# Making a unit's second diagonals on ScalarE instead of GpSimd, from unit 8 on

## The chip, the cores and the metric

The kernel runs on one core of one Trainium2 chip. Its time is the device time of one execution in microseconds (us), given as the median of three runs. A core has five engines that run their own instruction streams and meet only at semaphores: TensorE (PE in the profile, with its weight loads as PEld), VectorE (DVE), ScalarE (ACT), GpSimd (POOL) and SyncE (SP), which here only issues DMAs.

## The reference, cut to what matters

Four blocks are added one after the other to `x` (4 batches, 256 rows, 256 columns): a recurrence, a quantised feed-forward layer, a grouped attention over two sets of keys, and a routed linear attention. The change lies in the third block, whose core is:

```python
def _gqa(q, k, v):
    scale = 1.0 / np.sqrt(q.shape[-1])
    scores = jnp.einsum('bsghd,btgd->bghst', q, k) * scale
    p = jax.nn.softmax(scores, axis=-1)
    return jnp.einsum('bghst,btgd->bsghd', p, v)

q = _ln(_fp8_linear_pertensor(ln_out, wq, ...)); k = _ln(...); v = ...
core = _gqa(q, k, v)            # x = 0 in the kernel
qx = _ln(...); kx = _ln(...); vx = ...
xout = _gqa(qx, kx, vx)         # x = 1 in the kernel
```

There are 4 batches with 8 groups of 2 heads each, and each group has both attentions.

## The kernel before, in words

A **unit** is one group of one batch; there are 32, numbered 0 to 31, and unit u = 8 b + g. Within a unit `x` is 0 for the first attention and 1 for the second, and `t` is one of two tiles of 128 rows. The order of the work is written out by hand, one list for each engine; nothing is reordered. An engine that waits holds up everything behind it in its own list.

What a unit's second half of the pipeline does:

- `guard(u, x)` on TensorE (L700) makes scores in bfloat16, only to find the largest score of each row; `maxima(u, x, t)` on VectorE (L1852) takes the negated maximum into `nm`.
- `diagonals(u, x)` (L1426) turns `nm` into four 128x128 diagonal matrices in `diag`, by multiplying an identity matrix `identb` with the maximum of each row. In the kernel before, GpSimd makes all of them: one operation of 128x512 for x = 0 and one for x = 1.
- `scores(u, x, t)` on TensorE makes the real scores transposed (L714) and adds the diagonals through a matmul with ones (L715), which subtracts the row's maximum in every column. It waits for `diag_ready`.
- `exps(u, x, t)` on ScalarE (L1109) takes the exponentials, `weigh(u, x, t)` on TensorE (L734) multiplies with the values, and `outputs(u, x, t)` on VectorE (L1865, L1867) divides by the sums into `Cb`.
- `quantise(u - 1)` on VectorE (L1879 to L1883) rounds the unit before to 8 bits in five operations over 128x1024 elements.

Beside this runs the start of the next unit: `project(u + 1, t)` on TensorE (L590 and L597), `squares` and `values` on ScalarE (L1126, L1116), `powers` on GpSimd (L1409, L1411), `normalise` on VectorE (L1840, L1844), `turn` on TensorE (L673) and `evacuate` on ScalarE (L1150). Spread over the eight units of a batch lies the work of the first two blocks of the next batch, and from unit 25 on some preparation of the fourth block.

TensorE's list for a plain unit is scores(u, 0, 0), scores(u, 0, 1), project(u + 1, 1), scores(u, 1, 0), weigh(u, 0, 0), turn_outputs(u - 1), scores(u, 1, 1), weigh(u, 0, 1), turn(u + 1), weigh(u, 1, 0), project_values(u + 2), guard(u + 1, 0), weigh(u, 1, 1), project(u + 2, 0), guard(u + 1, 1). The last unit, 31, has no next one: its four scores stand directly behind each other.

Of the kernel before, what the change touches and what calls it, by code (L numbers as in the profile page):

```python
# [7 lines left out]
ALU = mybir.AluOpType  # L8
ACT = mybir.ActivationFunctionType
# [34 lines left out]
def build_program(nc, a, out):  # L44
# [15 lines left out]
    NT, KT = S // P, D // P  # L60
    HEADS = a["L1_xattn_wq"].shape[0] // P
    G = a["L1_xattn_wk"].shape[0] // P
    HPG = HEADS // G
# [10 lines left out]
    with main:  # L74
# [3 lines left out]
        def sb(name, shape, dt=F32, stack=main):  # L78
            return stack.enter_context(nc.sbuf_tensor(name, shape, dt))
# [7 lines left out]
        identb = sb("identb", [P, P], BF16)  # L87
# [69 lines left out]
        nm = [eb(f"nm{i}", [P, 2, HPG, NT]) for i in range(2)]  # L157
        diag = [eb(f"diag{i}", [P, 2, HPG * NT, P], BF16) for i in range(2)]
# [126 lines left out]
        def heads(buffer, l):  # L285
# [19 lines left out]
            "xq_ready xqT_done xqT_evac ffn_done ffn_read zT_done lnT_evac y4_ready xq4_ready "  # L305

            "qkv_done q1_done v_ready ss_ready root_ready rs_ready norm_done tr_done qt_evac smax_done "
            "max_ready diag_ready st_done exp_done pv_done o_evac cq_ready cT2_done catT_evac proj_done x3_ready "

            "ve3_ready pw3_ready h3_ready h3T_done h3T_evac conv_ready silu_ready proj3_done gate3_done qkv3_evac g3_evac rotated "  # L310
            "th_done sq_ready vs_ready sd_ready sd_done wv3_ready wk3_ready head_rstd_ready og_ready o_ready last_o_ready oT_done oT_evac out_done "
# [3 lines left out]
        s = {n: sem(n) for n in names.split()}  # L315
# [154 lines left out]
        def _(pe):  # L470
# [233 lines left out]
            def scores(u, x, t):  # L704

                n = 4 * u + 2 * x + t
                o = SB[n % 2]
                free(o)
                if n >= 2:
                    pe.wait_ge(s["exp_done"], n - 1)  # L710
                if t == 0:
                    pe.wait_ge(s["qt_evac"], 4 * (u + 1))
                    pe.wait_ge(s["diag_ready"], 2 * u + x + 1)
                nc.tensor.matmul(o[:], KTt[u % 2][:, x, t * P:(t + 1) * P], QT[u % 2][:, x, :], start=True, stop=False)  # L714
                nc.tensor.matmul(o[:], onesb[:], diag[u % 2][:, x].rearrange("p a b -> p (a b)"), start=False, stop=True  # L715
                                 ).then_inc(s["st_done"], 1)
# [260 lines left out]
            u = UNITS - 1  # L977
# [43 lines left out]
        def _(act):  # L1021
            A = nc.scalar.activation
# [80 lines left out]
            def exps(u, x, t):  # L1103

                n = 4 * u + 2 * x + t
                act.wait_ge(s["st_done"], n + 1)
                if u:
                    act.wait_ge(s["pv_done"], 4 * (u - 1) + 2 * x + 2)
                A(Pt[:, x, t], SB[n % 2][:], ACT.Exp, scale=SCALE).then_inc(s["exp_done"], 1)  # L1109

            def values(u, t):

                act.wait_ge(s["qkv_done"], 4 * u + 2 * t + 2)
                if u >= 2 and t == 0:
                    act.wait_ge(s["pv_done"], 4 * (u - 1))
                A(V[u % 2][:, :, t, 0:P], QB[2 * t + 1][:].rearrange("p (x j c) -> p x j c", x=2, j=2)[:, :, 1, :], ACT.Copy  # L1116
                  ).then_inc(s["v_ready"], 1)
# [125 lines left out]
            for u in range(UNITS - 1):  # L1243
                nb, steps = ahead(u)
                exps(u, 0, 0)
                if u == 0:
                    turned_h(1)
                if u >= SCORES_FIRST:
                    exps(u, 0, 1)
                if 7 in steps and u < G:  # L1250
                    over_scales(nb, (0, 1))
                if u + 1 == G:
                    squares(u + 1, 0)
                    values(u + 1, 0)
                    for r in round_of(u, 0):
                        weights(*r)
                squares(u + 1, 1)
                values(u + 1, 1)
                if 7 in steps and u >= G:
                    over_scales(nb, (0, 1))  # L1260
                if 1 in steps:
                    turned_context(nb)
                if 5 in steps:
                    turned_xq(nb)
                if u < SCORES_FIRST:
                    exps(u, 0, 1)
                exps(u, 1, 0)
                if u >= 1 and not (u % G == 1 and u > G) and 4 not in steps:
                    outputs(u - 1)
                exps(u, 1, 1)  # L1270
                if 4 in steps:
                    outputs(u - 1)
                for r in round_of(u, 1 if u + 1 == G else 0):
                    weights(*r)
                if 1 in steps:
                    differences(nb, 0, 1)
                evacuate(u + 1, range(3))
                if u % G == 1 and u > G:
                    outputs(u - 1)
                evacuate(u + 1, (3,))  # L1280
                if 7 in steps and u >= G:
                    over_scales(nb, (2, 3))
                for r in round_of(u, 2 if u + 1 == G else 1):
                    weights(*r)
                if 7 in steps and u < G:
                    over_scales(nb, (2, 3))
                if 1 in steps:
                    differences(nb, 2, 3)
                if 6 in steps and u < G:
                    turned_z(nb)  # L1290
                if u + 2 != G and u + 2 < UNITS:
                    squares(u + 2, 0)
                    values(u + 2, 0)
                if 0 in steps:
                    turned_h(nb)
                if 6 in steps and u >= G:
                    turned_z(nb)
                if u + 1 != G:
                    for r in round_of(u, 2):
                        weights(*r)  # L1300

            u = UNITS - 1
            exps(u, 0, 0)
            exps(u, 0, 1)
            exps(u, 1, 0)
            exps(u, 1, 1)
            outputs(u - 1)
# [36 lines left out]
        def _(pool):  # L1344
# [76 lines left out]
            def diagonals(u, x):  # L1421

                pool.wait_ge(s["max_ready"], 4 * u + 2 * x + 2)
                if u >= 2 and x == 0:
                    pool.wait_ge(s["st_done"], 4 * (u - 1))
                gp.tensor_tensor(diag[u % 2][:, x], identb[:].unsqueeze(1).to_broadcast([P, HPG * NT, P]),  # L1426
                                 nm[u % 2][:, x].rearrange("p h t -> p (h t)").unsqueeze(2).to_broadcast([P, HPG * NT, P]),
                                 ALU.mult).then_inc(s["diag_ready"], 1)

            inv_freq = (1.0 / np.float32(10000.0) ** (np.arange(0, DK3, 2, dtype=np.float32) / np.float32(DK3))).astype(np.float32)  # L1430
            for l in range(B):
# [54 lines left out]
            for u in range(UNITS):  # L1486
                nb, steps = ahead(u)
                diagonals(u, 0)
                if u + 1 != G and u + 1 < UNITS:
                    powers(u + 1, 0)  # L1490
                diagonals(u, 1)
                if 2 in steps:
                    weighted_values(nb)
                if u + 1 == G:
# [61 lines left out]
        def _(dve):  # L1556
# [290 lines left out]
            def maxima(u, x, t):  # L1847

                dve.wait_ge(s["smax_done"], 4 * u + 2 * x + t + 1)
                if u >= 2 and x == 0 and t == 0:  # L1850
                    dve.wait_ge(s["diag_ready"], 2 * (u - 1))
                v.tensor_reduce(nm[u % 2][:, x, :, t], GUARD_BANK[t][:].rearrange("p (h t) -> p h t", h=HPG), AX_X, ALU.max,  # L1852
                                negate=True).then_inc(s["max_ready"], 1)

# [295 lines left out]
            u = UNITS - 1  # L2150
# [75 lines left out]
```

## Time and profile before

| | us |
|---|---|
| median of 3 runs (range) | 662.53 (662.47 to 662.95) |
| the profiled execution's own time | 662.35 |
| its span, first to last instruction | 660.4 |
| TensorE busy | 610.7 |
| VectorE busy | 542.9 |
| ScalarE busy | 402.8 |
| GpSimd busy | 255.9 |

The span lies 1.95 us under the execution's own time, and that is 0.18 us under the median. Busy times of the engines overlap. A matmul's end is modelled by the profile, so two matmuls of one list can seem to overlap; distances between starts are the safer reading.

### The profile page before, as it was taken

To read this page: it belongs to the slowest core of one execution; us is meant where nothing else is said; L and a number is where in the kernel's file an instruction comes from. 1 tells how busy PE (TensorE), PEld (TensorE's weight loads), DVE (VectorE), ACT (ScalarE), POOL (GpSimd) and SP (SyncE) were. 2 spreads that over 40 slices of the span, in tenths; PEclk is the share of its full clock that TensorE was granted. 3 is DMA by queue.
4 is the path that set the end of the run, shared out by engine and by line. 5 is a ranking of instruction groups with operands and counts; after the bars stand their busy time and mean duration, and the time that the engine had idled before them with its cause. 6 is when DMAs were issued, how large, how long until landed. Compare 5 with 4: busy or idle time off the path is not lost.

```text
span 660.4 us, 13262 instructions
## 1 busy us (share of the span) xinstructions
PE 610.7 (92%) x4526; PEld 490.9 (74%) x4567; DVE 542.9 (82%) x1284; ACT 402.8 (61%) x1355; POOL 255.9 (39%) x344
## 2 busy tenths in 40 slices
PE   3567999999899999999999999999999999999957
PEld 2456787777678887787788877887887888887735
DVE  6999788989797879898878798889775777868697
ACT  4468866766676645667567466576553656665632
POOL 2213664343433543343345533333332444431281
PEclk9558999999999999999999999999999999999977
DMA  8486752330653203333343232333342233010001
GB/s 273 141 290 196 244 172 81 100 100 6 222 190 100 106 14 105 103 105 108 103 122 105 94 105 105 104 105 105 106 167 105 105 105 104 17 34 1 1 0 64
DMA packets 36972, 72.86 MB, mean 110 GB/s; under 512 B 3342, under 2 KB 28586, under 8 KB 32810
## 3 DMA queue, kind: packets, MB, share of 16 engines
q1 hardware_dynamic: 36720, 72.00, 33.5%
q8 instruction: 37, 0.61, 0.4%
q14 instruction: 29, 0.24, 0.1%
q10 hardware_dynamic: 186, 0.02, 0.0%
HBM read 59.41 MB, written 12.60 MB: 109 GB/s over the span
## 4 chain that ended last, share of the span: by engine, by line
PE 67%; DVE 25%; issue 4%; ACT 3%; POOL 1%; DMA 0%; POOLq 0%; DVEq 0%
PE bank L734 14%; PE bank L714 13%; PE bank L590 12%; PE bank L597 7%; PE bank L673 4%; PE bank L700 3%; DVE nm L1852 3%; PE bank L758 3%; PE bank L715 2%; DVE Cb L1867 2%; PE bank L748 2%; PE bank L480 1%; PE bank L771 1%; DVE Ce L1880 1%; DVE big L2016 1%
## 5 line engine op out<-in xcount | busy, mean ns | idle before, releaser
L1126 ACT ACTIVATE square<-bank 128x128 bf16<-128x128 f32 x372 | 97.7, 280 | 87.3 <-PE bank L590 72.8
L734 PEld LDWEIGHTS bank<-V,Pt 128*128 128x128 f32 x1024 | 128.2, 191 | 27.0 <-DVE Cb L1867 13.6
L734 PE MATMUL bank<-V,Pt 128*128 128x129 f32 x1024 | 136.3, 276 | 3.7 <-DVE Cb L1867 3.1
L714 PE MATMUL bank<-QT,KTt 128*128 128x512 f32 x256 | 132.5, 599 | 2.0 <-POOL diag L1426 0.3
L1426 POOL TENSOR_TENSOR diag<-identb,nm 128x512 bf16<-128x512 bf16 x64 | 67.7, 1058 | 168.3 <-DVE nm L1852 168.1
L1109 ACT ACTIVATE Pt<-bank 128x512 f32<-128x512 f32 x128 | 76.7, 599 | 67.0 <-remote 37.7
L1852 DVE TENSOR_REDUCE nm<-bank 128x2 f32<-128x512 f32 x128 | 82.3, 684 | 19.6 <-PE bank L700 19.3
L1411 POOL TENSOR_TENSOR rs<-ve,mhalf 128x6 f32<-128x6 f32 x62 | 87.9, 1417 | 5.2
L1867 DVE SCALAR_TENSOR_TENSOR Cb<-bank,ro,ism 128x128 bf16<-128x128 f32 x256 | 78.0, 346 | 4.5
L590 PE MATMUL bank<-WQ,xq 128*128 128x256 f32 x512 | 79.2, 297 | 1.4 <-DVE xq L1761 0.8
L1126 ACT ACTIVATION_READ_ACCUMULATOR square<-bank 128x1 f32 x372 | 78.1, 210 | 0.0
L590 PEld LDWEIGHTS bank<-WQ,xq 128*128 128x128 f32 x512 | 66.8, 189 | 14.6 <-DVE nm L1852 7.0
L597 PE MATMUL bank<-WC,vT 128*128 128x256 f32 x256 | 69.5, 396 | 0.7 <-ACT WC L1096 0.7
L1865 DVE RECIPROCAL ro<-bank 128x2 f32<-128x2 f32 x128 | 21.1, 165 | 56.8 <-PE bank L734 56.6
L1150 ACT ACTIVATE QT<-bank,vec 128x512 f32<-128x512 f32 x64 | 50.1, 783 | 19.8 <-PE bank L673 19.8
L1409 POOL TENSOR_SCALAR ve<-ss 128x6 f32<-128x6 f32 x62 | 17.9, 288 | 112.6 <-ACT square L1126 112.6
L590 PE MATMUL bank<-WH,xh 128*128 128x128 bf16 x768 | 54.1, 220 | 1.5 <-DVE xh L1761 1.5
L714 PEld LDWEIGHTS bank<-QT,KTt 128*128 128x128 f32 x256 | 43.0, 190 | 14.7 <-issue 11.4
L597 PEld LDWEIGHTS bank<-WC,vT 128*128 128x128 f32 x256 | 44.9, 195 | 4.6 <-ACT WC L1096 0.9
L590 PEld LDWEIGHTS bank<-WH,xh 128*128 128x128 bf16 x768 | 43.1, 98 | 4.7 <-DVE xh L1761 1.9
L673 PE MATMUL bank<-ident,Qn 128*128 128x128 f32 x372 | 45.7, 273 | 0.0
L1158 ACT ACTIVATE catT<-bank 128x1024 bf16<-128x1024 bf16 x32 | 32.8, 1024 | 18.7 <-PE bank L748 18.7
(241 smaller groups left out, 1052.0 us busy)
## 6 DMA issues: line engine op xcount, KB each, us to landing
WQ<-wq_split SPq DMA_DIRECT2D x24, 1024.0 KB, 7.7
WH<-wh_split SPq DMA_DIRECT2D x24, 384.0 KB, 8.9
wq_split<-WQ SPq DMA_DIRECT2D x8, 1024.0 KB, 5.2
ism<-smooth_inverse SPq DMA_DIRECT2D x32, 256.0 KB, 6.4
wpst<-in_L_xattn_wproj SPq DMA_DIRECT2D x16, 256.0 KB, 4.6
wh_split<-WH SPq DMA_DIRECT2D x8, 384.0 KB, 5.1
wst<-in_L_xattn_wq SPq DMA_DIRECT2D x8, 256.0 KB, 4.8
wst<-in_L_xattn_wqx SPq DMA_DIRECT2D x8, 256.0 KB, 5.0
```

Of the source, the lines that this page charges most:

```text
L590: last = nc.tensor.matmul(o[:, o0:o0 + n], x, w, start=m == 0, stop=m == parts * KT - 1)
L597: last = nc.tensor.matmul(QB[2 * t + 1][:, 2 * P:4 * P], vT[b % 2][:, k, t * P:(t + 1) * P], WC[:, k, g, :], start=k == 0, stop=k == KT - 1)
L673: last = nc.tensor.transpose(o[:, (j * NT + t) * P:(j * NT + t + 1) * P], Qn[:, t, h, :], ident[:])
L714: nc.tensor.matmul(o[:], KTt[u % 2][:, x, t * P:(t + 1) * P], QT[u % 2][:, x, :], start=True, stop=False)
L734: last = nc.tensor.matmul(o[:, h * (P + 2):h * (P + 2) + P + 1], Pt[:, x, k, h * S + t * P:h * S + (t + 1) * P], V[u % 2][:, x, k, 0:P + 1 ...
L1109: A(Pt[:, x, t], SB[n % 2][:], ACT.Exp, scale=SCALE).then_inc(s["exp_done"], 1)
L1126: last = A(square[:, t, h], head(t, h), ACT.Square, accum_out=ss[:, t, h:h + 1])
L1150: A(o, i, ACT.Identity, scale=vc(f"L1_xattn_{name}ln_w"), bias=vc(f"L1_xattn_{name}ln_b")).then_inc(s["qt_evac"], 1)
L1411: gp.tensor_tensor(rs[:, t, :], ve[:, t, :], mhalf[:, 0:6], ALU.pow).then_inc(s["rs_ready"], 1)
L1426: gp.tensor_tensor(diag[u % 2][:, x], identb[:].unsqueeze(1).to_broadcast([P, HPG * NT, P]), nm[u % 2][:, x].rearrange("p h t -> p (h t)") ...
L1852: v.tensor_reduce(nm[u % 2][:, x, :, t], GUARD_BANK[t][:].rearrange("p (h t) -> p h t", h=HPG), AX_X, ALU.max, negate=True).then_inc(s["ma ...
L1867: last = v.scalar_tensor_tensor(out=c4[:, t, x, h, :], in0=o[:, h * (P + 2):h * (P + 2) + P], scalar=ro[:, x, t, h:h + 1], in1=ism[:, u % ...
```

## The change

For units 8 to 31 the diagonals of x = 1 are made by ScalarE in four operations of 128x128, each a copy of the identity matrix with the column of negated maxima as its scale. They stand in ScalarE's list behind exps(u, 0, 1) and ahead of squares(u + 1, 1); in unit 31 they stand between exps(31, 0, 1) and exps(31, 1, 0). GpSimd keeps the diagonals of x = 0 for all units and those of x = 1 for units 0 to 7. The one semaphore `diag_ready` becomes two, `diag0_ready` and `diag1_ready`.

```diff
@@ TensorE, scores
-                    pe.wait_ge(s["diag_ready"], 2 * u + x + 1)
+                    pe.wait_ge(s[f"diag{x}_ready"], u + 1)
@@ ScalarE
+            def diagonals(u):
+
+                act.wait_ge(s["max_ready"], 4 * u + 4)
+                act.wait_ge(s["st_done"], 4 * (u - 1))
+                for h in range(HPG):
+                    for t in range(NT):
+                        last = A(diag[u % 2][:, 1, h * NT + t, :], identb[:], ACT.Copy, scale=nm[u % 2][:, 1, h, t:t + 1])
+                last.then_inc(s["diag1_ready"], 1)
...
                 if u >= SCORES_FIRST:
                     exps(u, 0, 1)
+                if u >= G:
+                    diagonals(u)
...
             u = UNITS - 1
             exps(u, 0, 0)
             exps(u, 0, 1)
+            diagonals(u)
             exps(u, 1, 0)
             exps(u, 1, 1)
@@ GpSimd
-                                 ALU.mult).then_inc(s["diag_ready"], 1)
+                                 ALU.mult).then_inc(s[f"diag{x}_ready"], 1)
...
-                diagonals(u, 1)
+                if u < G:
+                    diagonals(u, 1)
@@ VectorE, maxima
-                if u >= 2 and x == 0 and t == 0:
-                    dve.wait_ge(s["diag_ready"], 2 * (u - 1))
+                if u >= 2 and t == 0:
+                    dve.wait_ge(s[f"diag{x}_ready"], u - 1)
```

ScalarE's list in unit 22, before. `Pt` is what exps writes, `square` what squares writes, `V1` what values writes:

```order
L1109 ACTIVATE Pt<-bank4 128x512 [waits pv_done,st_done]
L1109 ACTIVATE Pt<-bank5 128x512 [waits pv_done,st_done]
L1126 ACTIVATE square,ss<-bank2 128x128 [waits rs_ready,qkv_done]
L1126 ACTIVATE square,ss<-bank2 128x128 x3
L1126 ACTIVATE square,ss<-bank3 128x128 [waits qkv_done]
L1126 ACTIVATE square,ss<-bank3 128x128
```

The same place after the change; line numbers behind L1110 have moved by 9:

```order
L1109 ACTIVATE Pt<-bank4 128x512 [waits pv_done,st_done]
L1109 ACTIVATE Pt<-bank5 128x512 [waits pv_done,st_done]
L1117 ACTIVATE diag0<-identb,nm0 128x128 [waits st_done,max_ready]
L1117 ACTIVATE diag0<-identb,nm0 128x128 x3
L1135 ACTIVATE square,ss<-bank2 128x128 [waits rs_ready,qkv_done]
L1135 ACTIVATE square,ss<-bank2 128x128 x3
L1135 ACTIVATE square,ss<-bank3 128x128 [waits qkv_done]
L1135 ACTIVATE square,ss<-bank3 128x128
```

Four operations have come between the second exponential and the first squares, and with them a wait for all four maxima of the unit.

ScalarE's list in unit 31, before:

```order
L1109 ACTIVATE Pt<-bank4 128x512 [waits pv_done,st_done]
L1109 ACTIVATE Pt<-bank5 128x512 [waits pv_done,st_done]
L1109 ACTIVATE Pt<-bank4 128x512 [waits pv_done,st_done]
L1109 ACTIVATE Pt<-bank5 128x512 [waits pv_done,st_done]
L1158 ACTIVATE catT<-bank7 128x2x512 [waits cT2_done]
```

and after:

```order
L1109 ACTIVATE Pt<-bank4 128x512 [waits pv_done,st_done]
L1109 ACTIVATE Pt<-bank5 128x512 [waits pv_done,st_done]
L1117 ACTIVATE diag1<-identb,nm1 128x128 [waits st_done,max_ready]
L1117 ACTIVATE diag1<-identb,nm1 128x128 x3
L1109 ACTIVATE Pt<-bank4 128x512 [waits pv_done,st_done]
L1109 ACTIVATE Pt<-bank5 128x512 [waits pv_done,st_done]
L1167 ACTIVATE catT<-bank7 128x2x512 [waits cT2_done]
```

Here the diagonals of x = 1 stand behind the exponentials of x = 0, where GpSimd made them beside these.

GpSimd's list over units 30 and 31, before (`rs` is what powers makes):

```order
L1426 TENSOR_TENSOR diag0<-identb,nm0 128x512 [waits st_done,max_ready]
L1409 TENSOR_SCALAR ve<-ss 128x6 [waits norm_done,ss_ready]
L1411 TENSOR_TENSOR rs<-ve,mhalf 128x6 [waits pool_chain]
L1426 TENSOR_TENSOR diag0<-identb,nm0 128x512 [waits max_ready]
L1409 TENSOR_SCALAR ve<-ss 128x6 [waits norm_done,ss_ready]
L1411 TENSOR_TENSOR rs<-ve,mhalf 128x6 [waits pool_chain]
L1426 TENSOR_TENSOR diag1<-identb,nm1 128x512 [waits st_done,max_ready]
L1426 TENSOR_TENSOR diag1<-identb,nm1 128x512 [waits max_ready]
```

and after:

```order
L1438 TENSOR_TENSOR diag0<-identb,nm0 128x512 [waits st_done,max_ready]
L1421 TENSOR_SCALAR ve<-ss 128x6 [waits norm_done,ss_ready]
L1423 TENSOR_TENSOR rs<-ve,mhalf 128x6 [waits pool_chain]
L1421 TENSOR_SCALAR ve<-ss 128x6 [waits norm_done,ss_ready]
L1423 TENSOR_TENSOR rs<-ve,mhalf 128x6 [waits pool_chain]
L1438 TENSOR_TENSOR diag1<-identb,nm1 128x512 [waits st_done,max_ready]
```

One operation of 128x512 in each unit is gone from the list, 24 in all; the rest has kept its order.

## Rows read from the trace of the kernel before

**Rows 1.** The page, part 1: busy us, share of the span, instructions.
```profile
PE 610.7 (92%) x4526; PEld 490.9 (74%) x4567; DVE 542.9 (82%) x1284; ACT 402.8 (61%) x1355; POOL 255.9 (39%) x344
```

**Rows 2.** Timeline of TensorE: start, us, line, operands, count, [idle before].
```profile
385.25 1.22 PE L590 MATMUL bank<-WQ,xq 128*128 128x256 f32 x8
397.50 1.19 PE L590 MATMUL bank<-WQ,xq 128*128 128x256 f32 x8
...
434.45 1.30 PE L590 MATMUL bank<-WQ,xq 128*128 128x256 f32 x8
...
445.96 1.20 PE L590 MATMUL bank<-WQ,xq 128*128 128x256 f32 x8
450.38 1.21 PE L590 MATMUL bank<-WQ,xq 128*128 128x256 f32 x8
...
457.85 1.16 PE L734 MATMUL bank<-V,Pt 128*128 128x129 f32 x8 [1.10 <-DVE Cb L1867]
...
463.17 1.19 PE L590 MATMUL bank<-WQ,xq 128*128 128x256 f32 x8
```

**Rows 3.** The chain that ended last, in unit 16: start, us, what.
```profile
343.76 0.44 PE bank L480 x4
```

**Rows 4.** Timeline of VectorE, units 18 and 22.
```profile
386.16 1.20 DVE L1880 TENSOR_SCALAR Ce<-Cb 128x1024 uint16<-128x1024 uint16 x1
...
450.84 0.42 DVE L1879 TENSOR_SCALAR Cb<-Cb 128x1024 bf16<-128x1024 bf16 x1
451.30 1.15 DVE L1880 TENSOR_SCALAR Ce<-Cb 128x1024 uint16<-128x1024 uint16 x1
```

**Rows 5.** Line 1880 alone: duration in ns, min/median/max, first and last start.
```profile
L1880 DVE TENSOR_SCALAR Ce<-Cb x32: 426/429/1202, 84.8 to 607.9; 128x1024 uint16<-128x1024 uint16 x32
```

**Rows 6.** Timeline of GpSimd, unit 22.
```profile
451.00 1.15 POOL L1426 TENSOR_TENSOR diag<-identb,nm 128x512 bf16<-128x512 bf16 x1
```

**Rows 7.** Timeline of ScalarE, unit 21.
```profile
434.84 0.60 ACT L1109 ACTIVATE Pt<-bank 128x512 f32<-128x512 f32 x1 [0.48 <-PE bank L715]
435.79 0.28 ACT L1126 ACTIVATE square<-bank 128x128 bf16<-128x128 f32 x1 [0.35 <-PE bank L590]
...
437.40 0.28 ACT L1126 ACTIVATE square<-bank 128x128 bf16<-128x128 f32 x1 [0.47 <-PE bank L597]
...
438.17 1.71 ACT L1050 ACTIVATE tmp<-tmp,vec 128x256 bf16<-128x256 f32 x4
439.77 0.60 ACT L1109 ACTIVATE Pt<-bank 128x512 f32<-128x512 f32 x1
```

**Rows 8.** Timeline of TensorE's weight loads, unit 21.
```profile
436.98 0.41 PEld L714 LDWEIGHTS bank<-QT,KTt 128*128 128x128 f32 x2
```

**Rows 9.** Timeline of ScalarE, in the first batch.
```profile
130.03 1.14 ACT L1092 ACTIVATE WH<-bank,vec 128x128 bf16<-128x128 f32 x4
```

**Rows 10.** Groups by line and form: count, busy us, mean ns, idle before.
```profile
L1109 ACT ACTIVATE Pt<-bank 128x512 f32<-128x512 f32 x128 | 76.7, 599 | 67.0 <-remote 37.7 <-PE bank L715 26.4
...
L1116 ACT ACTIVATE V<-bank 128x256 f32<-128x256 f32 x64 | 25.5, 398 | 0.0
```

**Rows 11.** Timeline of ScalarE, unit 31.
```profile
599.38 0.60 ACT L1109 ACTIVATE Pt<-bank 128x512 f32<-128x512 f32 x1 [0.48 <-PE bank L715]
```

**Rows 12.** The chain that ended last, from unit 31 on.
```profile
598.10 1.02 PE bank L714 x2
599.12 0.22 PE bank L715
599.34 0.86 PE bank L714 x2
600.20 0.21 PE bank L715
...
617.45 0.93 PE bank L864 x4
```

**Rows 13.** Busy time in stretches: PE, PEld, DVE, ACT, POOL, granted clock, DMA.
```profile
594.00:600.00 6.00, 5.86 (x32) 3.51 (x33) 5.86 (x13) 1.47 (x3) 2.19 (x2) 1.00 0.00 0
...
636.00:642.00 6.00, 0.00 (x0) 0.00 (x0) 5.74 (x11) 1.76 (x3) 5.37 (x9) 0.57 0.00 0
642.00:648.00 6.00, 4.97 (x15) 3.77 (x16) 5.83 (x9) 1.29 (x3) 3.70 (x4) 0.50 0.00 1
```

More of the change, by code:

```diff
@@ L307, in build_program @@
             "qkv_done q1_done v_ready ss_ready root_ready rs_ready norm_done tr_done qt_evac smax_done "
-            "max_ready diag_ready st_done exp_done pv_done o_evac cq_ready cT2_done catT_evac proj_done x3_ready "
+            "max_ready diag0_ready diag1_ready st_done exp_done pv_done o_evac cq_ready cT2_done catT_evac proj_done x3_ready "
             "ve3_ready pw3_ready h3_ready h3T_done h3T_evac conv_ready silu_ready proj3_done gate3_done qkv3_evac g3_evac rotated "
```

## The prediction

> **What bounds the kernel now.** I read the busy shares first. TensorE is busy for 92% of the span [rows 1], so time can be saved only where it stands still, and it is lost wherever TensorE is made to stand still. Then I looked for such places in units 8 to 31, by the distance between the starts of equal matmuls in TensorE's timeline. From the second project of a unit to the first project of the next-but-one there are 11.51 us in a plain unit: 434.45 to 445.96 in unit 21 [rows 2]. In unit 22 the same list takes 12.79 us, 450.38 to 463.17, though no matmul is added; 1.28 us are lost. The row at 457.85 shows where: weigh(22, 0, 1) waits for VectorE's output. In unit 18 it is 12.25 us, 385.25 to 397.50 [rows 2]; four transposes belong to that unit alone, at 0.44 us [rows 3], so 12.25 - 11.51 - 0.44 = 0.30 us are lost. Units 14 and 10 repeat 22 and 18 one batch earlier, with the same distances. Elsewhere in units 8 to 31 I find next to nothing lost behind the second diagonals.
>
> Then VectorE in those units. It works without a pause in unit 22, and one operation of quantise sticks out: L1880 took 1.15 us at 451.30, in unit 18 it took 1.20 us at 386.16 [rows 4], while its median over the kernel is 0.43 [rows 5]. GpSimd was making the second diagonals meanwhile, from 451.00 to 452.15 [rows 6], and L1880 ends 0.30 us behind that. L1879, just ahead, took 0.42 us beside a ScalarE exponential. So a fast operation of VectorE stands still while GpSimd's operation runs, and not while ScalarE's does.
>
> The Trainium skill has a rule for this: "GPSIMD Engine Reference", section on specifications, says that GpSimd's interfaces to SBUF are shared with VectorE, with contention against instructions in a two-port mode or with two SBUF inputs. The trace agrees for L1880, by the 1.15 us above against 0.43.
>
> **What the change removes.** 24 GpSimd operations of some 1.04 to 1.15 us. GpSimd is busy for 39% [rows 1] and nobody waits there, so this by itself is worth 0; what stood behind it in GpSimd's list, powers(u + 1, 1) and in units 9 and 17 a product for the next batch, may start 1 us earlier, where TensorE loses nothing. With each goes a stall of VectorE of about 0.72 us (1.15 - 0.43), some 17 us of VectorE's time. TensorE collects it only where it waits behind that stall:
> - units 14 and 22: the stall of 0.72 is smaller than the 1.28 us lost, so all of it counts: 2 x 0.72 = 1.44 us;
> - units 10 and 18: 0.77 (1.20 - 0.43) is more than the 0.30 lost, so TensorE becomes the limit and only 0.30 counts: 2 x 0.30 = 0.60 us;
> - the 20 other units: TensorE does not wait behind this stall, 0.
>
> Saved: 2.04 us. The bound below is 0 (another wait takes the place at once), the bound above is all that is lost in the four, 2 x 1.28 + 2 x 0.30 = 3.2 us.
>
> **What the change adds: the length of the four copies.** The trace has no operation of just this form. The nearest is L1050, a copy from SBUF to SBUF in bfloat16 with a scale from a column, but of 256 columns: four took 1.71 us [rows 7]. The exponentials of 512 columns take 599 ns and the values' copies of 256 take 398 [rows 10], so 128 columns are worth about 0.10 us, and four shorter copies take 1.71 - 4 x 0.10 = 1.31 us. L1092 has 128 columns and a scale column but reads PSUM; four took 1.14 us [rows 9]. I take 1.31, since its source lies in SBUF as here. Bounds: 1.14 below and 1.71 above. On ScalarE the next operation starts about 0.11 us before the last has ended (438.17 + 1.71 against 439.77 [rows 7]).
>
> **In units 8 to 30** the copies fall into a pause. In unit 21 the second exponential starts at 434.84 and takes 0.60; the squares start at 435.79, and the fifth square at 437.40 after another pause of 0.47 us, each time on TensorE's project [rows 7]. With the copies: they run from 435.33 to 436.64, the squares start at 436.53 instead of 435.79, four squares take about 1.0 us (436.53 to 437.53), and the fifth starts some 0.1 us late instead of waiting 0.47. Two who might wait: scores(u, 1, 0) needs the diagonals, and its weights are loaded at 436.98 [rows 8], 0.34 us behind their end; and GpSimd's powers, VectorE's normalise and TensorE's turn hang on the squares, late by 0.1 us, where VectorE had other work to do first. The maxima that the copies wait for are made about when the second exponential is done. Cost 0 each; with copies of 1.71 us in all they would end at 437.04, still about when the weights are loaded, so 0 to 0.1 each.
>
> The new wait of maxima(u, 1, 0) on VectorE, ahead of all its later work, is for diagonals of two units ago, some 30 us old: 0.
>
> **In unit 31** there is no project between the scores, and this cover is gone. Before, GpSimd made the diagonals beside the exponentials. Now exps(31, 0, 1) runs at 599.38 for 0.60 us [rows 11], the copies from 599.87 to 601.18, and about 0.06 us later TensorE may start scores(31, 1, 0), at 601.24. Its two matmuls then take 1.02 us as they do behind a wait (598.10 [rows 12]) and end at 602.26, where they ended at 599.34 + 0.86 = 600.20 before. Everything behind is late by 2.06 us, and nothing absorbs it: the chain of waits is TensorE without a gap from 599.34 to the row at 617.45 [rows 12], and goes on from its result. Bounds: 1.14 makes it 1.89, 1.71 makes it 2.46.
>
> **The sum.** -2.04 + 0 + 2.06 = +0.02 us. The profiled execution has 662.35 us, so 662.37; the median of the runs stood 0.18 above it, so I forecast 662.5 us. The case's own range, from the bounds that go together, is 661.2 (3.2 saved, 1.89 lost) to 663.6 (1.44 saved, 2.46 lost).
>
> **Rivals.**
> - *Another wait takes the place, and the last unit pays alone.* VectorE's stall goes in unit 22, but TensorE then waits there as long for the exponentials or for the squares that ScalarE now makes later. Against it: ScalarE had pauses of 0.48, 0.35 and 0.47 us in such a unit [rows 7]. Time: 662.53 + 2.06 = 664.6. This is slower. Chance 0.10.
> - *The copies outlast the window in every unit.* From the second exponential's start to the weights of scores(u, 1, 0) there are 436.98 - 434.84 = 2.14 us [rows 7, 8]; 0.49 go to the exponential, so the copies may take 1.65 us, 0.41 each. Beyond that TensorE waits in each of the units 8 to 30, 23 at most. At 1.85 us: 23 x 0.2 = 4.6, and 2.6 in unit 31, less 2.04: 667.7. Four operations of 128 columns in 1.14 us, 0.29 each, speak against it [rows 9]. Chance 0.04.
> - *The clock falls in unit 31.* The granted clock is 1.00 from 594 to 600, and fell to 0.57 and 0.50 of full speed (the lower level, 1.2 GHz, is 0.50) in the stretches from 636 and from 642, after TensorE had done nothing for 6 us [rows 13]. The new pause in unit 31 is near 2 us, longer than the 1.10 us at 457.85 and shorter than that one. If the clock fell for 6 us, TensorE would do half the work in them, about 3 us more: 665.5. Chance 0.04.
> - *The tail takes it in.* The last unit's wait is hidden, since VectorE and ScalarE behind it have pauses, and the savings stand alone: 662.53 - 2.04 = 660.5. The gapless chain [rows 12] speaks against it. Together with savings at their upper bound that I have not found the places for, chance 0.12.
> - *The change does nothing*, if VectorE's stall is not GpSimd's doing and the last unit's copies are hidden by something: 662.5, the same number; it lies within the chance of the first case.
>
> The rule that speaks loudest against this change is that of the clock: the Trainium skill, "TensorE: Matmul & The Clock Gate", part 1, says that a monitor halts every second pulse when TensorE has not been busy lately. The trace agrees by the 0.57 behind the idle stretch from 636; by the rule the third rival's time would be right only if the new pause counts as idle, and no run here shows one of 2 us.
>
> **How the numbers follow.** What a measurement of this kernel can tell from no change is 0.2%, 1.3 us, so faster means under 661.2 and slower over 663.9. The forecast has 0.70, and nearly all of it lies within. The faster rival gives 0.12. The slower ones give 0.10 + 0.04 + 0.04 = 0.18. The range takes in the first rival's 664.6 above and, below, a little more than the case's own bound of 661.2: 661.0 to 664.6, with under 0.2 left outside.
>
> **What would show it.** The second operation of quantise on VectorE, L1880 before, at 0.43 us in nearly every unit from 8 on. The project distance of units 14 and 22 near 12.07 instead of 12.79, of units 10 and 18 near 11.95. ScalarE's four copies at about 1.3 us in the pause behind the second exponential, with the fifth square starting at most 0.1 us behind TensorE. TensorE idle for 1.9 to 2.5 us ahead of the third scores of unit 31, released by ScalarE, and the clock at 1.00 there. I am wrong if TensorE waits for ScalarE's diagonals in other units, if unit 22 stays at 12.79, or if the last unit shows no new pause.

## The result, and the profile after

Over 20 runs of each kernel the changed one takes 664.75 us (663.18 to 666.68) and the one before 662.54 us (662.44 to 664.40). The ratio is 1.0035 with a 95% interval of 1.0024 to 1.0046: slower by 2.2 us, where I had forecast 662.5 and at most 664.6. The 20 runs stand in three levels, which the explanation needs: five lie at 663.18 to 663.30, seven at 664.67 to 664.81, eight at 666.22 to 666.68. The profiled execution took 664.69 us.

Part 1 of its page, against [rows 1]:

```profile
PE 610.6 (92%) x4526; PEld 489.9 (74%) x4567; DVE 525.3 (79%) x1284; ACT 426.2 (64%) x1451; POOL 230.1 (35%) x320
```

VectorE lost 542.9 - 525.3 = 17.6 us of busy time with the same 1284 instructions, GpSimd 25.8 us with 24 fewer. The stalls went as forecast. Line numbers of VectorE stand 13 further on in this kernel (they move by 9 only in ScalarE's part): L1893 is L1880 of before, and L1880 is the old L1867. The same places as [rows 4], VectorE's timeline in units 18 and 22 (start, us, line, operands):

```profile
385.46 0.43 DVE L1893 TENSOR_SCALAR Ce<-Cb 128x1024 uint16<-128x1024 uint16 x1
...
450.48 0.43 DVE L1893 TENSOR_SCALAR Ce<-Cb 128x1024 uint16<-128x1024 uint16 x1
```

The second operation of quantise, L1893 now, takes 0.43 where it took 1.20 and 1.15. In the kernel before, each of the units 8 to 31 had exactly one lengthened operation of quantise beside the second product of GpSimd, but not always this one: it was L1880 in 11 units, L1881 in 3 and L1882 in 10. So the sign that I had named, L1880 at 0.43, held in 13 of the 24 units already before; the sum of 17.6 us is the better sign. In unit 21 of the kernel before the lengthened one was L1882, whose median is 0.69:

```profile
434.38 1.41 DVE L1882 TENSOR_TENSOR Cb<-Cb,Ce 128x1024 bf16<-128x1024 bf16 x1
```

TensorE's timeline in the changed kernel, beside [rows 2]:

```profile
384.55 1.22 PE L590 MATMUL bank<-WQ,xq 128*128 128x256 f32 x8
396.69 0.48 PE L590 MATMUL bank<-WQ,xq 128*128 128x256 f32 x2
...
449.57 1.21 PE L590 MATMUL bank<-WQ,xq 128*128 128x256 f32 x8
...
456.31 1.16 PE L734 MATMUL bank<-V,Pt 128*128 128x129 f32 x8 [0.38 <-DVE Cb L1880]
461.64 1.19 PE L590 MATMUL bank<-WQ,xq 128*128 128x256 f32 x8
```

Unit 22 takes 12.07 us (12.79 before) and the wait for VectorE is 0.38 (1.10 before): 0.72 us won, as forecast; unit 14 won 0.71. Unit 18 takes 12.14 us (12.25 before): 0.11 won, where I had 0.30; unit 10 won 0.10. Together these are 1.64 us.

ScalarE in unit 21, the place of [rows 7]:

```profile
434.03 0.60 ACT L1109 ACTIVATE Pt<-bank 128x512 f32<-128x512 f32 x1 [0.48 <-PE bank L715]
434.52 1.26 ACT L1117 ACTIVATE diag<-identb,nm 128x128 bf16<-128x128 bf16 x4
435.69 0.26 ACT L1135 ACTIVATE square<-bank 128x128 bf16<-128x128 f32 x1
...
436.69 0.29 ACT L1135 ACTIVATE square<-bank 128x128 bf16<-128x128 f32 x1
```

The four copies take 1.26 us (forecast 1.31) and lie in ScalarE's pause. The fifth square, at 436.69, starts 2.66 us behind the second exponential where it was 2.56 [rows 7]: 0.10 late, as forecast. The view of line 1117 alone (duration in ns min/median/max, first and last start; then who waited for it, us and times) says that TensorE waited for it once in 24 units:

```profile
L1117 ACT ACTIVATE diag<-identb,nm x96: 386/390/403, 210.5 to 599.2; 128x128 bf16<-128x128 bf16 x96
...
  PE bank L714: 1.9, 1
```

That once is unit 31. ScalarE's and then TensorE's timeline there:

```profile
597.86 0.60 ACT L1109 ACTIVATE Pt<-bank 128x512 f32<-128x512 f32 x1 [0.47 <-PE bank L715]
598.36 1.26 ACT L1117 ACTIVATE diag<-identb,nm 128x128 bf16<-128x128 bf16 x4
```

```profile
599.76 1.44 PE L714 MATMUL bank<-QT,KTt 128*128 128x512 f32 x2 [1.94 <-ACT diag L1117]
600.99 0.63 PE L715 MATMUL bank<-diag,onesb 128*128 128x512 bf16 x1
601.42 1.91 PE L714 MATMUL bank<-QT,KTt 128*128 128x512 f32 x2
603.13 0.63 PE L715 MATMUL bank<-diag,onesb 128*128 128x512 bf16 x1
603.55 1.18 PE L734 MATMUL bank<-V,Pt 128*128 128x129 f32 x8
604.57 0.61 PE L748 MATMUL bank<-identb,Cb 128*128 128x128 bf16 x8
```

The pause of 1.94 us is the one that I worked out. What follows it is not: the two pairs of L714 behind the wait take 1.44 and 1.91 us, where the same pairs behind the same wait take 1.10 and 1.02 at full clock (experiment 9), and L715 takes 0.63 instead of 0.38. The stretches of this time (PE, PEld, DVE, ACT, POOL busy, then the granted clock) say why:

```profile
600.00:602.00 2.00, 2.00 (x4) 0.80 (x4) 0.00 (x0) 0.33 (x1) 0.00 (x0) 0.60 0.00 0
602.00:604.00 2.00, 2.00 (x6) 0.93 (x5) 0.00 (x0) 0.46 (x2) 0.00 (x0) 0.55 0.00 0
604.00:606.00 2.00, 2.00 (x24) 1.99 (x23) 1.09 (x5) 1.18 (x2) 0.00 (x0) 1.00 0.00 0
```

Finer stretches of the same trace have 0.50 (the lower level, 1.2 GHz) or 1.00 (2.4 GHz), and a value between them where the clock changes within the stretch. At 0.60 and 0.55 the clock was at the lower level for (0.40 + 0.45) x 2.00 / 0.50 = 3.4 us. The finer ones put this at 600.4 to 603.8: the first matmuls behind the pause, from 599.76, still ran at full clock. From the chain that ended last (start, us, what), against the 617.45 of [rows 12]:

```profile
598.36 1.27 ACT diag L1117 x4
...
599.76 1.44 PE bank L714 x2
...
619.80 0.93 PE bank L864 x4
```

The end of unit 31's work is late by 619.80 - 617.45 = 2.35 us, which is the whole difference of the two profiled executions (664.69 - 662.35 = 2.34). At unit 30's start the changed kernel was 1.52 us ahead (584.10 before, 582.58 after: 1.64 saved less 0.12 by which the first units of the two executions differ), so unit 31 cost 2.35 + 1.52 = 3.87 us. The pause's part is read from an execution with full clock (the faster one of experiment 9): there weigh(31, 0, 0) starts 6.55 us behind the unit's first scores, before it was 4.37, so the pause and its restart cost 2.18 us. The other 1.7 us are the clock's.

### The profile page after: what moved, and what is told of

It is laid out like the page before. It is cut to its first block, busy times and chain, and to the rows that moved or that the text cites. A ratio compares the mean times of both kernels' runs of the same rounds, so it can differ in the third digit from the quotient of the medians.

```text
span 662.7 us, 13383 instructions
## 1 busy us (share of the span) xinstructions
PE 610.6 (92%) x4526; PEld 489.9 (74%) x4567; DVE 525.3 (79%) x1284; ACT 426.2 (64%) x1451; POOL 230.1 (35%) x320
## 4 chain that ended last, share of the span: by engine, by line
PE 70%; DVE 21%; issue 4%; ACT 3%; POOL 1%; DMA 0%; DVEq 0%; POOLq 0%; ACTq 0%
PE bank L734 15%; PE bank L714 14%; PE bank L590 13%; PE bank L597 7%; PE bank L673 5%; PE bank L700 3%; PE bank L758 3%; DVE nm L1865 2%; PE bank L715 2%; PE bank L748 2%; DVE Cb L1880 1%; PE bank L480 1%; PE bank L771 1%; DVE big L2029 1%; DVE WQ L1836 1%
## 5 line engine op out<-in xcount | busy, mean ns | idle before, releaser
L714 PE MATMUL bank<-QT,KTt 128*128 128x512 f32 x256 | 133.8, 604 | 3.9 <-ACT diag L1117 1.9
L1438 POOL TENSOR_TENSOR diag<-identb,nm 128x512 bf16<-128x512 bf16 x40 | 42.0, 1050 | 164.9 <-DVE nm L1865 164.9
L1880 DVE SCALAR_TENSOR_TENSOR Cb<-bank,ro,ism 128x128 bf16<-128x128 f32 x256 | 78.1, 347 | 4.5
L1421 POOL TENSOR_SCALAR ve<-ss 128x6 f32<-128x6 f32 x62 | 15.8, 254 | 138.1 <-ACT square L1135 138.1
L714 PEld LDWEIGHTS bank<-QT,KTt 128*128 128x128 f32 x256 | 43.2, 191 | 17.3 <-issue 14.7
```

Of the source, the lines that this page charges most:

```text
L1880: last = v.scalar_tensor_tensor(out=c4[:, t, x, h, :], in0=o[:, h * (P + 2):h * (P + 2) + P], scalar=ro[:, x, t, h:h + 1], in1=ism[:, u % ...
```

## The experiments

The theory was: 1.64 us are saved by VectorE's stalls in four units; the pause in unit 31 costs about 2.1; behind it the clock falls in most executions and takes about 1.6 more. The rivals: the copies also cost something small in each of the 23 other units, or the time lies in something that all runs share. Each experiment ran beside more runs of the kernel before. These too have an upper level, some 1.9 us above the rest: 2 of the 20 runs of the result lie there, 7 of 23 beside experiments 1 to 4, 15 of 34 beside experiments 5 to 8. A median moves with that share, so I compare the lowest levels as well.

**1. GpSimd keeps the last unit.**

```diff
@@ ScalarE, unit 31
-            diagonals(u)
@@ GpSimd
-                if u < G:
+                if u < G or u + 1 == UNITS:
                     diagonals(u, 1)
```

> Units 8 to 30 as in the change, unit 31's second diagonals by GpSimd as before. Theory A (the savings of VectorE's stall are real, 1.6 us by the project distances of units 10, 14, 18 and 22; all of the loss, pause and slow clock, lies in unit 31): 660.9 us, narrow, no pause over 0.5 us in unit 31, clock 1.00 there. Rival B (the copies on ScalarE cost something in other units too, or the slow clock comes from the body of the kernel): 662.5 or more, and a wide spread as the changed kernel has.

660.98 us (12 runs, eight of them at 660.83 to 661.07), ratio to the kernel before 0.998 [0.997, 0.999]. The other four, at 662.52 to 662.89, go against my "narrow". None of them was profiled, and they stand 1.6 to 2.0 us up with no pause in unit 31, so a step of this size in a time does not by itself say which fall it was. No pause is left in unit 31:

```profile
597.37 0.38 PE L715 MATMUL bank<-diag,onesb 128*128 128x512 bf16 x1
597.58 1.02 PE L714 MATMUL bank<-QT,KTt 128*128 128x512 f32 x2
```

The sign turns with this one unit, and 23 units of copies on ScalarE cost nothing that shows. This version beats both kernels, by 1.6 and by 3.8 us of the medians and by 1.6 and 2.3 of the lowest levels.

**2. ScalarE makes only the last unit's.**

```diff
@@ ScalarE, units 8 to 30
-                if u >= G:
-                    diagonals(u)
...
@@ GpSimd
-                if u < G:
+                if u + 1 < UNITS:
                     diagonals(u, 1)
```

> Only unit 31's second diagonals by ScalarE, all others by GpSimd. Theory A: the pause alone is 2.1 us, so no run lies under 664.6, and in some runs the clock falls behind it for 3.4 us and adds 1.7 (666.3), or more in others (about 668): three levels as in the changed kernel, each 1.5 us higher. Rival B: the loss in unit 31 is only a part; 663 to 664, narrow.

665.0 us (6 runs: 664.5 to 665.15 four times, 666.51, 666.56), ratio 1.0037 [1.0024, 1.0051]. The pause stands alone: the lowest run, 664.5, is the 662.35 of the profiled execution before plus 2.15. In its profiled execution, this same run, the same wait of 1.94 us left the clock at full speed, and the matmuls behind it took 1.10 us for two:

```profile
601.35 1.10 PE L714 MATMUL bank<-QT,KTt 128*128 128x512 f32 x2 [1.94 <-ACT diag L1117]
```

So the pause does not always bring the clock down. Four of the six runs lie below the 666.0 that a fall would give, and the two at 666.5 lie 2.0 us up, about where the kernel before has its own upper level (1.8 to 2.0 us up). At most two of six runs can have had the fall here, against 15 of 20 of the changed kernel with the same wait; I expected the same three levels as there.

**3. The copies ahead of the exponentials in unit 31.**

```diff
             u = UNITS - 1
+            diagonals(u)
             exps(u, 0, 0)
             exps(u, 0, 1)
-            diagonals(u)
```

> As the change, but in unit 31 ScalarE makes the four copies ahead of the exponentials of x = 0, in the 4 us in which it waits. Theory A: the first exponential starts some 0.4 us late, TensorE's pause is 0.2 to 0.4 us, the clock stays at 1.00: 661.1 to 661.4, narrow. Rival B (any work of ScalarE between the scores of unit 31 costs its length, 1.3 us, wherever it stands): 662.3 or more.

662.04 us (12 runs: six at 661.16 to 661.34, six at 662.73 to 663.15), ratio 0.9984 [0.9973, 0.9995]. ScalarE begins them when the maxima are there, and the exponentials follow:

```profile
596.09 1.28 ACT L1117 ACTIVATE diag<-identb,nm 128x128 bf16<-128x128 bf16 x4 [3.37 <-DVE nm L1865]
597.27 1.15 ACT L1109 ACTIVATE Pt<-bank 128x512 f32<-128x512 f32 x2
```

TensorE's third scores start at 597.90 against 597.58 in experiment 1. The order in ScalarE's list was most of the price: the same four copies, ahead of two exponentials instead of behind them, give back 663.2 - 661.2 = 2.0 us between the lowest levels, and 664.75 - 662.04 = 2.7 us between the medians. What they still cost is 661.18 - 660.86 = 0.3 us of the profiled executions. I did not profile its upper runs; they may be either clock fall of experiment 9.

**4. Other matmuls in the pause.** Five parts of the last projection, with no tie to unit 31, are moved from behind its weigh to between its second and third scores.

```diff
@@ TensorE, unit 31
             scores(u, 0, 1)
+            project_last(0, (3, 4, 5))
+            project_last(1, (0, 1))
             scores(u, 1, 0)
...
-            project_last(0, (3, 4, 5, 6))
-            project_last(1, (0, 1, 2, 3))
+            project_last(0, (6,))
+            project_last(1, (2, 3))
```

> As the change, but 20 matmuls of the output projection (L771, 2.2 us) stand between scores(31, 0, 1) and scores(31, 1, 0) instead of behind the unit, so TensorE works while ScalarE makes the copies. Theory A: the wait is covered, no clock fall: 660.9 to 661.2, narrow. Rival C (the clock falls for another reason than the pause, such as what the matmuls of unit 31 are): low clock and a wide spread stay, 662 to 664.

665.07 us (6 runs: four at 664.73 to 665.35, two at 666.54 and 666.57), ratio 1.0038 [1.0025, 1.0052]: my expectation was 4 us too low. TensorE's timeline shows the pause filled, and another of about the same length further on:

```profile
599.51 2.35 PE L771 MATMUL bank<-WP,catT 128*128 128x256 bf16 x20
601.69 1.02 PE L714 MATMUL bank<-QT,KTt 128*128 128x512 f32 x2
...
612.77 0.76 PE L748 MATMUL bank<-identb,Cb 128*128 128x128 bf16 x8 [2.07 <-DVE Cb L1898]
```

The moved matmuls had covered the wait for the last unit's quantise. In unit 31 the scores, exponentials, outputs and quantise are a chain of dependent steps, and the copies are in it; work to fill the gap only moves the gap. The slow clock moved with it (0.72 over 612 to 618). The profiled execution, 666.57, is of the upper pair and has the second fall of experiment 8 too.

**5. Two copies ahead of the exponentials, two behind.**

```diff
@@ ScalarE, unit 31
+            diagonals(u, (0,))
             exps(u, 0, 0)
             exps(u, 0, 1)
-            diagonals(u)
+            diagonals(u, (1,))
```

> As the change, but in unit 31 ScalarE makes two of the four copies ahead of the exponentials and two behind them. Theory A (each copy behind the exponentials costs its own length in TensorE's pause, and the clock falls behind a pause the more often the longer it is): pause 1.4 us instead of 1.94, fastest runs at 662.6 (0.6 under the changed kernel's 663.18), and fewer runs 1.5 above that. Rival (a fall has nothing to do with the pause's length): as many raised runs as in the changed kernel, 15 of 20.

662.53 us (12 runs: nine at 662.32 to 662.62, three at 664.15 to 664.38), ratio 0.9992 [0.9981, 1.0003].

```profile
599.06 1.10 PE L714 MATMUL bank<-QT,KTt 128*128 128x512 f32 x2 [1.36 <-ACT diag L1117]
```

The pause is paid: 662.32 is 1.5 us above the 660.86 of experiment 1's profiled execution. The profiled execution has full clock. The three upper runs were not profiled. They stand where 15 of 34 runs of the kernel before, which has no such pause, stand beside this experiment (663.96 to 664.47), so they are more likely the second fall of experiment 8 than one behind this pause; that is not shown. Either way at most 3 of 12 runs had a fall here, against 15 of 20.

**6. Every copy twice in unit 31,** the first four to a tile that nobody reads.

```diff
@@ ScalarE, unit 31
-            diagonals(u)
+            diagonals(u, 2)
```

> As the change, but in unit 31 ScalarE makes four copies into a spare tile ahead of the four that count, so the pause of TensorE grows by their 1.17 us. Theory A: pause 3.1 us, fastest runs at 664.35, and the clock falls behind the pause in most or all runs (665.9 and more). Rival: fastest runs at 664.35, raised ones as rare as in the kernel before, 2 of 20.

667.02 us (11 runs; one took 807 us at a mean granted clock of 0.747, and without it the median is 666.48), ratio 1.0052 [1.0036, 1.0069], also without it. Two runs are at 664.3, where I expected the pause alone; the other eight are 1.6 to 4.8 us above. The wait (the scores' lines stand one further on here, L714 is L715) and the stretches around it:

```profile
600.89 2.04 PE L715 MATMUL bank<-QT,KTt 128*128 128x512 f32 x2 [3.11 <-ACT diag L1120]
```

```profile
600.00:602.00 2.00, 1.11 (x2) 0.62 (x3) 0.00 (x0) 0.75 (x3) 0.00 (x0) 0.50 0.00 0
602.00:604.00 2.00, 2.00 (x4) 0.70 (x3) 0.00 (x0) 0.60 (x1) 0.00 (x0) 0.50 0.00 0
604.00:606.00 2.00, 2.00 (x7) 1.20 (x6) 0.00 (x0) 0.47 (x1) 0.00 (x0) 0.50 0.00 0
606.00:608.00 2.00, 2.00 (x20) 1.99 (x20) 0.78 (x4) 0.59 (x2) 0.00 (x0) 0.81 0.00 0
```

Here the clock was at the lower level for 6.8 us, twice the 3.4 of the changed kernel, and it fell within the wait itself, at 599.9. This is one execution; whether every wait of 3.11 us does so is not shown.

**7. GpSimd makes a product for nobody.** This is experiment 1, and in units 8 to 30 GpSimd makes the same 128x512 product as before into a tile that nobody reads.

```diff
@@ GpSimd
...
+                else:
+                    pool.wait_ge(s["max_ready"], 4 * u + 4)
...
+                    chain.add(gp.tensor_tensor(spare[:], identb[:]..., nm[u % 2][:, 1]..., ALU.mult))
```

> Unit 31 by GpSimd (as the run of 660.98), and in units 8 to 30 GpSimd, besides ScalarE's copies, multiplies the same 128x512 into a spare tile that nobody reads, where it made the second diagonals before. Theory A (the saving is VectorE's stall beside GpSimd's operation): the stall is back, VectorE's second operation of quantise takes 1.15 us again, and the time is 662.5, as before. Rival (the saving comes from something else, such as when scores(u, 1, 0) or powers may start): 660.9.

662.52 us (12 runs: nine at 662.34 to 662.63, three at 663.79 to 664.31), ratio 0.999 [0.998, 1.0001]; 1.5 us above experiment 1, and VectorE's operation is long again:

```profile
451.06 0.41 DVE L1898 TENSOR_SCALAR Cb<-Cb 128x1024 bf16<-128x1024 bf16 x1
451.50 1.15 DVE L1899 TENSOR_SCALAR Ce<-Cb 128x1024 uint16<-128x1024 uint16 x1
```

Nobody waits for this product, so it does not cost by coming late itself. It could still cost by holding back powers, which stands behind it in GpSimd's list, and this edit brings that back too. The trace of the kernel before speaks against that: VectorE waited for powers' `rs` once in the whole kernel, for 0.7 us within the first 100 us. In unit 22 TensorE's wait for VectorE shrank by 0.72 us, the stall's length. So the cost goes through VectorE's stall; the prediction had argued this from two rows.

**8. ScalarE only in units 10, 14, 18 and 22.**

```diff
@@ ScalarE
-                if u >= G:
+                if u in (10, 14, 18, 22):
                     diagonals(u)
@@ ScalarE, unit 31
-            diagonals(u)
@@ GpSimd
-                if u < G:
+                if u not in (10, 14, 18, 22):
                     diagonals(u, 1)
```

> Second diagonals by ScalarE in units 10, 14, 18 and 22 alone, by GpSimd in all others. Theory A (only these four are worth anything, 0.10 + 0.71 + 0.11 + 0.72 us): 660.9 us, as with all of units 8 to 30. Rival (the other 19 add to it, or take from it): their part of 1.6 us is missing or more.

662.39 us (12 runs: five at 660.72 to 661.37, seven at 662.24 to 662.75), ratio 0.9979 [0.9968, 0.999]. The lower group equals that of experiment 1. Four units make all of the saving; the 19 others make none, as the prediction said. Its profiled execution is of the upper group and shows a clock fall in quite another place, in unit 6, where TensorE has the same short waits in every kernel. The kernel before has them too, of 1.57 and 0.69 us, and kept full clock behind them in its profiled execution. Here are the stretch from 160 to 174 us and the four matmuls that took 2.08 us, where they take 1.13 at full clock:

```profile
160.00:174.00 14.00, 11.74 (x83) 9.90 (x82) 9.85 (x32) 6.66 (x14) 4.68 (x5) 0.88 0.34 105
```

```profile
166.98 0.49 PE L561 MATMUL bank<-cen,wst 128*128 128x128 f32 x2 [1.57 <-DVE rest L1835]
...
168.60 2.08 PE L597 MATMUL bank<-WC,vT 128*128 128x256 f32 x4 [0.69 <-ACT WC L1096]
```

**9. The changed kernel again, four profiled executions,** to see which clock falls go with which level.

> The changed kernel as it is, profiled again, to see which stretches of slow TensorE clock go with which of its three levels (663.2, 664.7 and 666.6 us). Theory A (clock falls at two separate places, each of them in some executions): at a time near 663.2 the clock is 1.00 both at 160 to 176 us and at 600 to 604 us, near 664.7 only the second is slow, near 666.6 both are. Theory B (the levels are one effect of the whole run, such as memory or the start): the stretches of slow clock are the same at each level.

> The same kernel once more, for another of the three levels. Theory A: each slow stretch is worth what its level shows, 1.5 us at 600 to 604 us and 1.9 us at 160 to 176 us. Theory B: the same slow stretches at every level.

These two took 664.74 and 664.58 us, the middle level, with slow clock between 600 and 604.2 and none at 160 to 180. That left the other levels open.

> The changed kernel once more, since the two looks before both met the level of 664.7. Theory A: a run near 666.6 has slow clock at 160 to 176 us as well as at 600 to 604 us, a run near 663.2 at neither. Theory B: the early stretch shows 1.00 at 666.6 too, and the further 1.9 us lie elsewhere.

> The same kernel and the same two theories as in the run beside it: slow clock at 160 to 176 us only when the time is near 666.6, at 600 to 604 us unless it is near 663.2 (A), or no such relation (B).

These took 666.83 and 662.98 us, the two levels that were missing. In the slower one, TensorE's stretches at 170 and at 602 and 604 us:

```profile
170.00:174.00 4.00, 4.00 (x23) 3.61 (x22) 2.65 (x7) 0.49 (x2) 1.04 (x1) 0.63 0.69 178
...
602.00:604.00 2.00, 2.00 (x5) 0.89 (x6) 0.00 (x0) 0.60 (x1) 0.00 (x0) 0.77 0.00 0
604.00:606.00 2.00, 2.00 (x7) 1.21 (x6) 0.00 (x0) 0.56 (x1) 0.00 (x0) 0.50 0.00 0
```

In the faster one both places have full clock; its row from 170 and its timeline behind the pause:

```profile
170.00:174.00 4.00, 4.00 (x38) 3.42 (x37) 2.74 (x8) 2.66 (x15) 1.04 (x1) 1.00 0.51 145
```

```profile
599.76 1.10 PE L714 MATMUL bank<-QT,KTt 128*128 128x512 f32 x2 [1.94 <-ACT diag L1117]
600.69 0.38 PE L715 MATMUL bank<-diag,onesb 128*128 128x512 bf16 x1
600.91 1.02 PE L714 MATMUL bank<-QT,KTt 128*128 128x512 f32 x2
...
601.98 1.05 PE L734 MATMUL bank<-V,Pt 128*128 128x129 f32 x8
602.87 0.61 PE L748 MATMUL bank<-identb,Cb 128*128 128x128 bf16 x8
```

The kernel, the start at 599.76 and the wait of 1.94 are those of the first profiled execution. With full clock weigh starts at 601.98, with the slow clock at 603.55, and L748, which both reach at full clock, at 602.87 and 604.57. That is 1.70 us for the clock alone. The two executions differ by 664.69 - 662.98 = 1.71, and the levels of the 20 runs by 1.5. So in these five profiled executions the lowest level is neither fall, the middle one the fall in unit 31, the highest both.

## Why the prediction was wrong

**The step that failed** is the last term of the sum, +2.06 for unit 31, and in it the silent condition that is spelled out among the signs to look for: "and the clock at 1.00 there". I had the clock's fall as a rival with a chance of 0.04, because no row of the trace before had an idle TensorE of 2 us. What the runs showed in its place: of the changed kernel's 20 runs 15 stand at or above the level of that fall, and four of five profiled executions show it, with 3.4 us of slow clock and 1.7 us lost. In the terms of the sum: saved 1.64, pause 2.18, which gives the lowest level (662.54 - 1.64 + 2.18 = 663.1, seen 663.18), and 1.5 to 1.7 for the clock, which gives the median's 664.7. Without the clock the result would have lain in my range. The clock is 1.7 of the 2.2 us by which I was off; the rest are 0.40 saved too little in units 10 and 18 and 0.12 more for the pause. With all 2.04 us saved the median would have been near 664.4, inside the range by its edge, but still slower and not the no change that I had given 0.70. The sum put this term at nothing: it let the matmuls behind the pause run at their old length. The rival's price was too high in turn: it took 6 us of slow clock and 3 us lost.

The Trainium skill, "TensorE: Matmul & The Clock Gate", part 1, says of the slow matmuls at a kernel's start that their number changes from run to run of the same kernel. The runs here show the like in the middle of a kernel: the same 1.94 us cost the clock in one execution and not in another. I had weighed the rule only by whether it applies, when the question was in how many executions it does. With a chance of one half for that rival, the range would have reached to its 665.5 and held the time, and slower would have been as likely as no change.

**The level of 664.6** that I gave to the first rival lies near the measured 664.75 by luck: its mechanism, another wait in place of VectorE's, did not appear, and the savings came.

**Units 14 and 22** (2 x 0.72): right to 0.01 us, with the wait for VectorE down from 1.10 to 0.38.

**Units 10 and 18** (2 x 0.30): mis-sized; they gave 0.10 and 0.11. I said that "TensorE becomes the limit", and it does, but one step earlier than I thought. VectorE's timeline in unit 18:

```profile
389.91 0.17 DVE L1878 RECIPROCAL ro<-bank 128x2 f32<-128x2 f32 x1 [0.45 <-PE bank L734]
...
392.90 0.61 DVE L1880 SCALAR_TENSOR_TENSOR Cb<-bank,ro,ism 128x128 bf16<-128x128 f32 x2
```

VectorE, now 0.77 us earlier, waits 0.45 us for TensorE's product of weigh(18, 0, 0), and from there its list runs without a pause to the output that TensorE's next weigh needs. That weigh starts 393.57 - 384.55 = 9.02 us into the stretch instead of 9.13. The chain runs from TensorE through VectorE and back, and only the 0.11 us by which VectorE had lagged behind TensorE's product could be won.

**The 20 other units** and the copies in 8 to 30: right, by experiments 8 and 1. The copies' 1.31 us came out as 1.26, and the fifth square of unit 21 came 0.10 us late, as forecast.

**The pause in unit 31:** 2.18 us against 2.06 forecast. In the execution with full clock the third scores start 2.11 later and their first pair takes 0.07 more than before. That nothing behind absorbs it was right as well; experiment 4 shows how firmly.

**The other rivals.** That another wait takes the place in units 14 and 22, and that the copies outlast the window, fell by the distances above. That the tail takes the pause in fell by the chain and by experiment 2. That GpSimd was not the cause of the stall fell by experiment 7.

## What to carry to other kernels

Work of a helping engine that is hidden in the steady units has its own price in the last one, where the cover is gone and every step is on the chain: keep the old engine there, or put the new work ahead of what waits. When a change opens a pause of about 2 us in TensorE's work, count the pause, and beside it some 1.5 to 1.7 us for the clock that may fall behind it. Give that fall a real chance: by the levels of the times it came in 15 of 20 runs of one kernel and in at most two of six of another with the same wait. A stall that is removed pays only as far as the next thing that the freed engine waits for; follow that engine's list to the place before counting the whole of the loss.

## What the runs showed of the hardware

- TensorE's clock behind a wait in front of scores in unit 31: at 1.36 us no fall in the one profiled execution and at most 3 of 12 raised runs; at 1.94 us a fall in four of five profiled executions of one kernel (and none in the profiled execution of another with the same wait); at 3.11 us raised times in 8 of 10 runs and, in the one profiled, 6.8 us at the lower level. Each fall behind 1.94 us lasted 3.4 us and began 0.6 to 1.1 us after TensorE had started again. The step from 663 to 664.7 us in a list of times was such a fall.
- A second fall, in unit 6, goes with times some 1.9 us longer (660.8 and 662.7 in experiment 8; seen as slow clock in the profiles of experiments 4, 8 and 9), behind waits of 1.57 and 0.69 us within 2 us of each other. The fall itself takes 1.65 us of it: from the first L561 behind the wait to the next project there are 5.93 us in all three, and 4.28 or 4.29 in the executions with full clock. It stands ahead of unit 8, where the change begins. The upper level of the kernel before (2 of 20, 7 of 23 and 15 of 34 runs) is probably this fall; no profile of it shows that.
- GpSimd's 128x512 product of bfloat16 by a broadcast column lengthened one operation of quantise in each of the units 8 to 31 of the kernel before: those with one source, in bfloat16 or uint16, from 0.43 to 1.14 to 1.20 us, the one with two sources (L1882) from 0.69 to 1.41. ScalarE's copies of 128x128 out of the same tiles, 0.39 us each, did not (they run from 450.17 on, and L1893 has 0.43 at 450.48).
- What stays open: what decides between the two outcomes at 1.94 us. In unit 31 the start, the wait and the order were the same to 0.01 us in the execution with the fall and in that without. Open as well is why experiment 2, with the same wait 1.6 us later in the program, had the fall more rarely.
